# Attention on one core: where the halves of the weighing stand, and how the eight PSUM banks are shared between scores and maxima

## What is computed

```python
q = (src @ q_w).reshape(b, s, h, hd).transpose(0, 2, 1, 3)
k = (src @ k_w).reshape(b, s, h, hd).transpose(0, 2, 1, 3)
v = (src @ v_w).reshape(b, s, h, hd).transpose(0, 2, 1, 3)
scores = jnp.einsum('bhqd,bhkd->bhqk', q, k) / np.float32(np.sqrt(hd))
scale = jax.nn.sigmoid(jnp.einsum('bhsd,hd->bhs', q, scale_w)) * 2.0
scores = scores * scale[..., None]
aw = jax.nn.softmax(scores, axis=-1)
out = jnp.einsum('bhqk,bhkd->bhqd', aw, v)
```

## Time and profile before

| | us |
|---|---|
| median of three runs | 2585.01 |
| the profiled execution | 2593.07 |
| its span in the trace | 2591.3 |
| first and last start of a maximum | 718.3 and 2180.9 |
| first and last start of an exponential | 788.5 and 2233.8 |

### The profile page before, as it was taken

How to read it: one execution, slowest core, us unless ns; L and a number is a source line. 1 busy time by engine, 2 the same in 40 slices (tenths; PEclk the granted TensorE clock), 3 DMA queues, 4 the chain that set the end, 5 groups by cost and what they waited for, 6 DMA issues and landing times. The chain is left out here.

```text
span 2591.3 us, 49197 instructions
## 1 busy us (share of the span) xinstructions
PE 2472.1 (95%) x18379; PEld 1251.9 (48%) x18379; DVE 2124.7 (82%) x4155; ACT 1828.8 (71%) x2336; POOL 939.5 (36%) x1059
## 2 busy tenths in 40 slices
PE   7999999999789999999999999999999999997996
PEld 5566665555444444444444444444444444474654
DVE  6778888988767898988898898898899996183877
ACT  4888878777215777777777787777787777662664
POOL 1777878888600212111121121112101010155664
PEclk8999999999877999999999999999999999997998
DMA  3322323332430402204031040040030000125883
GB/s 106 122 80 85 104 88 93 98 101 85 106 63 18 65 19 46 38 18 50 18 48 20 18 66 3 17 66 18 18 50 2 2 1 24 39 86 182 300 281 113
DMA packets 96463, 178.70 MB, mean 69 GB/s; under 512 B 19382, under 2 KB 66150, under 8 KB 88400
## 3 DMA queue, kind: packets, MB, share of 16 engines
q1 hardware_dynamic: 89488, 160.43, 24.6%
q0 software_dynamic: 6016, 14.49, 1.6%
q10 hardware_dynamic: 720, 0.62, 0.1%
HBM read 145.11 MB, written 31.21 MB: 68 GB/s over the span
## 5 line engine op out<-in xcount | busy, mean ns | idle before, releaser
L1670 DVE TENSOR_REDUCE max_part<-round_psum 128x1 f32<-128x512 f32 x2048 | 1294.1, 686 | 167.2 <-PE round_psum L1577 136.0
L1634 ACT ACTIVATE p_exp<-score_psum 128x1024 f32<-128x1024 f32 x1024 | 1046.4, 1024 | 299.3 <-PE score_psum L1562 299.3
L1562 PE MATMUL score_psum<-q_stack,k_stack 50*128 50x512 f32 x2048 | 843.3, 475 | 4.7 <-ACT p_exp L1634 2.8
L1577 PE MATMUL round_psum<-k_stack,q_stack 48*128 48x512 f32 x2048 | 784.6, 461 | 9.6 <-DVE max_part L1670 5.6
L1609 PE MATMUL pv_psum<-p_exp,values 128*17 128x256 f32 x8192 | 644.4, 387 | 2.4 <-ACT pv_out L1650 0.3
L1562 PEld LDWEIGHTS score_psum<-q_stack,k_stack 50*128 50x128 f32 x2048 | 365.5, 184 | 482.9 <-issue 436.0
L1577 PEld LDWEIGHTS round_psum<-k_stack,q_stack 48*128 48x128 f32 x2048 | 314.5, 187 | 76.5 <-DVE max_part L1670 40.9
L672 PE MATMUL rot<-tokens_t,w_in 128*128 128x512 f32 x576 | 271.7, 602 | 0.4 <-DVE x_conv L839 0.2
L1609 PEld LDWEIGHTS pv_psum<-p_exp,values 128*17 128x17 f32 x8192 | 136.1, 95 | 271.5 <-issue 257.6
L1713 POOL TENSOR_TENSOR rden<-pv_out,minus_one 128x16 f32<-128x16 f32 x31 | 90.0, 2903 | 427.9 <-ACT pv_out L1653 424.9
L1700 POOL CAST max_parts<-max_neg 128x16 fp32r<-128x16 f32 x32 | 6.3, 198 | 463.2 <-DVE max_neg L1676 441.3
(11 more groups left out here) (296 smaller groups left out, 3320.2 us busy)
## 6 DMA issues: line engine op xcount, KB each, us to landing
cum_rows_in<-cum_rows SPq DMA_DIRECT2D x64, 512.0 KB, 3.9
expert_w<-in_expert_w SPq DMA_DIRECT2D x24, 1028.0 KB
qk_rows<-split_then_gate SPq DMA_DIRECT2D x64, 256.0 KB, 4.0
tokens_t<-in_expert_w SPq DMA_DIRECT2D x15, 1028.0 KB
cum_pairs_in<-cum_rows SPq DMA_DIRECT2D x240, 64.0 KB, 2.8
q_stack<-qk_rows SPq DMA_DIRECT2D x42, 256.0 KB, 12.7
k_stack<-qk_rows SPq DMA_DIRECT2D x42, 256.0 KB, 15.8
token_rows<-tokens SPq DMA_DIRECT2D x12, 512.0 KB, 7.5
```

The source lines that it names most:

```text
L1562: m = nc.tensor.matmul(ebank[i // 2][:, i % 2, :], ks[rows, n % 2, plane, k * P:(k + 1) * P], qs[rows, n % 2, plane, q * BLK:(q + 1) * BLK ...
L1577: nc.tensor.matmul(bank[step][:, :], qs[rows, n % 2, plane, at:at + P], ks[rows, n % 2, plane, keys * BLK:(keys + 1) * BLK], start=True, s ...
L1634: nc.scalar.activation(pt[:, (k * 2 + pair) % 4, :, :], ebank[pair][:, :, :], ACT.Exp).then_inc(*exped.up(u, k, pair))
L1670: nc.vector.tensor_reduce(mx[:, c * HG + h, keys:keys + 1], bank[step][:, :], AX_X, ALU.max).then_inc(*maxed.up(u, k, i))
```

## The change

The number of matmuls, reductions and bytes stays. Three things are changed.

1. Half 1 of the weighing of step t-2 moves from behind the first pair to behind the second, half 0 of step t-1 from behind the third to behind the fourth.
2. The scores get three single banks in a ring (`score_bank`) in place of two tiles of two banks: a score waits for the exponential of the score three places before it, whatever its head. Each score has its own exponential of 128x512 (2048 in place of 1024), its own `scored` and its own `exped`. The exponential of score 1 (and 3) waits for `weighed` of head pair 0 (and 1) of step t-2; those of scores 0 and 2 don't.
3. The ring of the maxima has four banks in place of three. The values of the first stage use one of them, so TensorE waits for their last copy (`first.v_stored`) before the first maximum and no longer at the first late value.

```diff
-            if left == ("max", 0) and 0 <= t - 2 < total:
+            if right == ("max", 1) and 0 <= t - 2 < total:
                 yield "weigh", *divmod(t - 2, KT), 1
-            if left == ("max", 2) and 0 <= t - 1 < total:
+            if right == ("max", 3) and 0 <= t - 1 < total:
                 yield "weigh", *divmod(t - 1, KT), 0
...
-    ebank = [ps(f"score_psum{i}", [P, 2, BLK]) for i in range(2)]
+    ebank = [ps(f"score_psum{i}", [P, BLK]) for i in range(3)]
...
-    rbank = [ps(f"round_psum{i}", [P, BLK]) for i in range(3)]
+    rbank = [ps(f"round_psum{i}", [P, BLK]) for i in range(4)]
...
-                                [ebank[0][:, i, :] for i in range(2)], [ebank[1][:, i, :] for i in range(2)], rbank[0:2],
+                                ebank[0:2], [ebank[2], rbank[3]], rbank[0:2],
...
-    bank = {u: rbank[i % 3] for i, u in enumerate(users)}
-    before = {u: users[i - 3] for i, u in enumerate(users) if i >= 3}
-
+    bank = {u: rbank[i % 4] for i, u in enumerate(users)}
+    before = {u: users[i - 4] for i, u in enumerate(users) if i >= 4}
+
+    scores = [(u, k, i) for u in range(NU) for k in range(KT) for i in (1, 0, 3, 2)]
+    score_bank = {score: ebank[i % 3] for i, score in enumerate(scores)}
+    score_before = {score: scores[i - 3] for i, score in enumerate(scores) if i >= 3}
...
-    scored = sems.events("scored", pairs)
-    exped = sems.events("exp_ready", pairs)
+    scored = sems.events("scored", scores)
+    exped = sems.events("exp_ready", scores)
...
+            pe.wait_ge(*first.v_stored)
...
-                    if i % 2 and (u, k) != (0, 0):
-                        pe.wait_ge(*exped.at(*back(u, k, 1), i // 2))
+                    if (u, k, i) in score_before:
+                        pe.wait_ge(*exped.at(*score_before[u, k, i]))
...
-                    m = nc.tensor.matmul(ebank[i // 2][:, i % 2, :], ks[rows, n % 2, plane, k * P:(k + 1) * P],
-                                         qs[rows, n % 2, plane, q * BLK:(q + 1) * BLK], start=True, stop=True)
-                    if i % 2 == 0:
-                        m.then_inc(*scored.up(u, k, i // 2))
+                    nc.tensor.matmul(score_bank[u, k, i][:, :], ks[rows, n % 2, plane, k * P:(k + 1) * P],
+                                     qs[rows, n % 2, plane, q * BLK:(q + 1) * BLK], start=True,
+                                     stop=True).then_inc(*scored.up(u, k, i))
...
-                            pe.wait_ge(*exped.at(u, k, h // 2))
+                            pe.wait_ge(*exped.at(u, k, h))
...
-                if what == "score" and i % 2 == 0:
+                if what == "score":
                     pair = i // 2
-                    act.wait_ge(*scored.at(u, k, pair))
-                    if (u, k) >= (0, 2):
+                    act.wait_ge(*scored.at(u, k, i))
+                    if i % 2 and (u, k) >= (0, 2):
                         act.wait_ge(*weighed.at(*back(u, k, 2), pair))
-                    nc.scalar.activation(pt[:, (k * 2 + pair) % 4, :, :], ebank[pair][:, :, :],
-                                         ACT.Exp).then_inc(*exped.up(u, k, pair))
+                    nc.scalar.activation(pt[:, (k * 2 + pair) % 4, i % 2, :], score_bank[u, k, i][:, :],
+                                         ACT.Exp).then_inc(*exped.up(u, k, i))
```

More of the change, by code:

```diff
@@ L1515, in v_bank @@
     def v_bank(c):
-        return ebank[c // 2 % 2][:, c % 2, 0:D]
+        return ebank[c % 3][:, 0:D]
     with nc.Block() as block:
@@ L1532, in _ @@
                 if what == "stack":
-                    stack_on_sync(nc, sp_, S, u, j, i, scored.at((u - 1) * SB - 1, KT - 1, 1) if u >= 2 else None)
+                    stack_on_sync(nc, sp_, S, u, j, i, scored.at((u - 1) * SB - 1, KT - 1, 2) if u >= 2 else None)
             sp_.wait_ge(*S.rest.at(len(GROUPS) - 1, SB - 1))
@@ L1583, in _ @@
                         pe.wait_ge(*first.src_t)
-                        pe.wait_ge(*first.v_stored)
-                    if c - 4 in late:
-                        pe.wait_ge(*v_stored.at(c - 4))
+                    if c - 3 in late:
+                        pe.wait_ge(*v_stored.at(c - 3))
                     for kd in range(KD):
```

## The result

| | us |
|---|---|
| changed kernel, median of four runs (2808.84 to 2815.26) | 2811.57 |
| kernel before, beside it on the same chip (2584.03 to 2588.49) | 2584.59 |
| ratio, with its 95% interval | 1.0876 (1.0857 to 1.0894) |
| profiled execution of the changed kernel (span 2809.0) | 2810.82 |

The change makes the kernel 227 us slower by the medians, and 218 us by the spans of the two profiled executions (2809.0 and 2591.3). Forecast were +208 us and 2793 us, within 2665 to 2870.

The account below looks back on a forecast made before the run. A closed loop of TensorE and ScalarE, 2.59 us a step, was taken as the bound, becoming 3.01. 207 + 4 + 12 - 10 - 5 = +208 us gave 2793 us, 8% slower, range 2665 to 2870.

Parts of the forecast that it names:

- The bound before: Attention steps of the kernel before: a closed loop of TensorE and ScalarE, 2.59 us a step, was taken as the bound.
- The new loop: Attention steps after the change: half 1, exponential of score 1, score 2, half 0, next step; 3.01 us against 2.59.
- score 2 stands ahead of half 0, which stands ahead of the next step: TensorE's order: score 2, waiting for the exponential of score 1, holds up the next step, closing the 3.01 us loop.
- 207 + 12 - 10 = +209 us: The 492 steps with maxima: +207 for the loop, +12 for the copy of `pv`, -10 for the maxima's fourth bank.
- the two ways to the 0.60 of an exponential: Exponential of 128x512: 597 ns from another function on that shape, and from 1024 less half a tile at 0.83 ns a column.
- 8 us more were taken off: Whole kernel: 2801 us from the profiled execution was lowered to 2793, as the median of runs lay 8 lower.
- 20 x 0.18 = +4: Last 20 steps, which have no maxima: the loop takes 2.78 us against 2.60, +4 us in all.
- the clock falls as well: Rival: TensorE's idle gaps lower its clock in a tenth of the 492 steps, +110 us, 2903 us; chance 0.05.
- I take -5, since the clock is low there and TensorE hardly gets ahead: Maxima ahead of the first score: one more filled bank hides some VectorE idling, -5 us, bounds 0 and -10.
- The fourth bank in the steps: Weight loads of maxima waited 41 us for VectorE; the fourth bank saves -10 us, bounds 0 and -41.
- The gain: Rival: the loop doesn't close, as score 1's exponential is in time for score 2; -89 us, 2496 us; chance 0.06.
- The shorter hold: Rival: from half 1 to score 1's exponential 0.41 us, not 0.71; 2.71 a step, +54, 2639 us; chance 0.08.

Follow-up runs that it names:

- the filled one: Changed kernel with three banks for the maxima, one bank unused, plus two matmuls of zeros ahead of each score 2 in the last 20 steps: 2812.13 us, ratio 1.0874.

## Why the prediction was right, and where it was not

**The bound before.** That TensorE and ScalarE closed a loop at 2.59 us, and not VectorE, holds: without changing VectorE's work the step fell to 2.44 in three ways (old places with single banks, new places alone, new places with four score banks).

**The new loop.** The step that decides, "score 2 stands ahead of half 0, which stands ahead of the next step", is shown. Its terms were 0.66, 0.71, 0.60 + 0.06, 0.42 and 0.56 and measured 0.67, 0.72, 0.65, 0.42 and 0.56. It vanishes if either end is undone: with the weighing moved back it is 2.44, with a fourth score bank 2.43. With half of the move undone the same sum gives 2.78 and 2.76, and 2.79 and 2.78 were measured. 207 + 12 - 10 = +209 us for the 492 steps came out as +214.5. (Of the two ways to the 0.60 of an exponential, the second is no second source: the 0.83 ns a column comes from the 597 ns that it is to confirm. The changed kernel's mean is 604 ns.)

**The total is closer than its terms.** In the spans it is +217.7 against +208, but by +20 in the last 20 steps, +5.5 in the 492 and +1 ahead of them, and by -11 and -6 in the two other stretches, which happen to pay back more than half. The forecast of 2793 us is 19 below the median because 8 us more were taken off, for the profiled execution of the kernel before, which lay above its median; that of the changed kernel took 2810.82 us with a median of 2811.57.

**"20 x 0.18 = +4" was mis-sized:** it measured +24.2. The loop there was right at first,

```profile
2383.25 0.63 PE L1611 MATMUL pv_psum<-p_exp,values 128*17 128x256 f32 x8
...
2386.03 0.63 PE L1611 MATMUL pv_psum<-p_exp,values 128*17 128x256 f32 x8
```

2.78 us a step, and then it was

```profile
2423.51 1.06 PE L1611 MATMUL pv_psum<-p_exp,values 128*17 128x256 f32 x8
...
2427.75 1.06 PE L1611 MATMUL pv_psum<-p_exp,values 128*17 128x256 f32 x8
```

4.24 us, at the lower level of the clock. The clock fell within 4 us, in the third step of the last unit:

```profile
2398.00:2400.00 2.00, 1.76 (x19) 0.64 (x19) 0.00 (x0) 1.23 (x4) 0.00 (x0) 1.00 0.00 0
2400.00:2402.00 2.00, 1.69 (x10) 0.44 (x9) 0.00 (x0) 2.00 (x4) 0.00 (x0) 0.58 0.00 0
2402.00:2404.00 2.00, 2.00 (x10) 1.00 (x6) 0.00 (x0) 0.57 (x2) 0.00 (x0) 0.50 0.03 8
```

Shortly before, at 2398.24, half 0 had waited 0.47 us for the copy of `pv`, on top of the gaps of each step. In the four other kernels whose clock fell in the last 20 steps it fell within about 2 us of that same half 0, also in the one with four score banks, though its steps there are only some 2.3 us long. The wait for the copy isn't what decides: with half 1 back the clock fell at 2263.4 us, just ahead of this half 0, which didn't wait at all, and with the new places alone TensorE waited 1.22 us for it and kept its clock. I had argued that the kernel before stands still there too and keeps its clock at 1.00. It does; what decides stays open, beyond that two more matmuls a step bring the clock back. The rival "the clock falls as well", to which I gave 0.05, therefore came true in one place, for 20 us and not for 110. The Trainium skill (TensorE: Matmul & The Clock Gate, A second HAM failure mode) warns of small idle gaps between groups of matmuls that rotate through PSUM banks; here the trace now agrees, for the last 20 steps, and for the 492 it does not: TensorE stood still for 0.32 us by the row of score 2 in those as well, and the clock stayed at 1.00.

**"I take -5, since the clock is low there and TensorE hardly gets ahead" was mis-sized too:** it measured -15.8, beyond my bound of -10. I had counted filled banks only. With four banks the clock itself is higher there, 0.86 to 0.90 in the five kernels with four, 0.69 to 0.73 in six of the seven with three. The seventh with three banks (the filled one) had 0.87 and took 59.9 us. So at like clocks the bank is worth 59.9 - 54.4 = 5.5 us, which is the -5 of the forecast, and the other 10 are the clock's; this rests on one execution. Why the clock is mostly higher with four banks isn't shown.

**The fourth bank in the steps:** -10 was taken, -5 was measured in the changed kernel, by one execution of each. The 41 us that weight loads of maxima waited for VectorE were a poor bound: in the changed kernel they wait 235 us, in 551 places, while the matmuls of the maxima themselves wait 1.0 us for VectorE. **The stretch behind attention** became 6.2 us shorter, which nothing in the sum answers to and no run was made for. In the twelve profiled executions it takes between 350.9 and 358.2 us, in the fastest kernel as little as in the slowest, so it is no mark of this change.

**The rivals.** The gain (0.06) would have needed the exponential within 0.23 us of half 1's start; it was 0.72. The shorter hold is out by the same row. The Trainium skill's rule that breaking instructions up may help where ScalarE isn't saturated but makes others wait (Perfetto Trace Analysis, Optimizing Scalar/DVE Operations) is borne out with the weighing in its old places: 1.5% faster with three banks for the maxima as before (ratio 0.9853). The small exponentials and the ring of three score banks came together there and weren't separated.

## What to carry to other kernels

Where a buffer ring, a hold and an order written by hand meet, write down the closed path from one step to the next and add its rows up: two edits that each open a loop can close another one together, and only the sum shows it. A ring's length decides which instruction inherits a wait; with a ring of three in a step of four scores, one held exponential reached the last score of its own step, with a ring of four it reached the next step. Try the parts of a change singly before it is given up: the new places and the new banks were each a gain.

## What the runs showed of the hardware

- TensorE's clock fell to its lower level in the last 20 steps of five of the twelve profiled executions, one of each kernel, and stayed at 1.00 in the others, though TensorE waits there in some of these too. Two matmuls of zeros in the gap of each step brought it back, for 17 us of net gain. Neither the length of the step decides (at about 2.3 us it fell in one kernel, at 2.60 it didn't in the kernel before) nor a wait for the copy of `pv` (it fell without one, and stayed up behind one of 1.22 us).
- A fourth bank for the maxima was worth 14 us to 16 us in a stretch where only maxima run, with the clock at 0.86 to 0.88 in place of 0.69 to 0.73; in the one execution with three banks and a clock of 0.87 it was 5.5 us.
- Exponentials of 128x512 follow each other 0.48 to 0.49 us apart, each 0.60 long: 2.06 for four in a row. Cutting 1024 of them in two cost nothing that shows in the kernels with the old places, where ScalarE was idle for 0.25 us a step.
